# Quantised feed-forward: the normalised row made by GpSimd one pass sooner, its maximum first on VectorE, statistics between the two products

## What is computed

```python
x = x + _L0_xattn_ref(_layernorm(x, axis=-1), ctx_512, L0_xattn_Wq, L0_xattn_Wkv, L0_xattn_Wo)
x = x + _L0_attn_ref(_layernorm(x, axis=-1), L0_attn_w_attn, ...)
x = x + _L0_ffn_ref(_layernorm(x, axis=-1), L0_ffn_w_gate, L0_ffn_w_up, L0_ffn_w_down)
x = x + _L1_xattn_ref(_layernorm(x, axis=-1), ctx_512, ctx_512, ...)
x = x + _L1_attn_ref(_layernorm(x, axis=-1), L1_attn_W, L1_attn_b)
x = x + _L1_ffn_ref(_layernorm(x, axis=-1), ...)          # 34 experts
```

```python
def _act_quant(x):
    scale = 127.0 / jnp.clip(jnp.max(jnp.abs(x), axis=-1, keepdims=True), 1e-05)
    xq = jnp.clip(jnp.round(x * scale), -128.0, 127.0) / scale
    return x + jax.lax.stop_gradient(xq - x)
def _bitlinear(x, w):
    return jnp.einsum('bsi,oi->bso', _act_quant(x), _weight_quant(w))
gate = jax.nn.silu(_bitlinear(x, w_gate))
up = _bitlinear(x, w_up)
return _bitlinear(gate * up, w_down)
```

## Time and profile before

| | |
|---|---|
| median of three runs | 1316.04 us (1314.11 to 1318.54) |
| profiled execution | 1316.23 us, span 1314.1 us |
| granted TensorE clock, mean over the span | 0.977 |
| TensorE busy (matmuls) | 1207.7 us, 92% of the span |
| VectorE busy | 800.6 us, 61% |
| ScalarE busy | 645.4 us, 49% |
| GpSimd busy | 559.3 us, 43% |
| quantised feed-forward, first maximum of `h` to the last addition to `X` | about 404.8 to 512.8 us |

### The profile page before, as it was taken

How to read it: one execution, slowest core, us unless ns; L and a number is a source line. 1 busy time by engine, 2 the same in 40 slices (tenths; PEclk the granted TensorE clock), 3 DMA queues, 4 the chain that set the end, 5 groups by cost and what they waited for, 6 DMA issues and landing times. The chain is left out here.

```text
span 1314.1 us, 30226 instructions
## 1 busy us (share of the span) xinstructions
PE 1207.7 (92%) x9768; PEld 949.2 (72%) x9776; DVE 800.6 (61%) x1775; ACT 645.4 (49%) x1374; POOL 559.3 (43%) x824
## 2 busy tenths in 40 slices
PE   6899999989996778988886899999999999999998
PEld 5677777767774446866664688888888788888886
DVE  4688888857766883658885854444444444444443
ACT  5766666634445885544444333444443443333443
POOL 2244444467774443547775233333332233333331
PEclk9999999989999997999997899999999999999999
DMA  8200000000001000200000133333333433333331
GB/s 280 57 17 16 16 16 8 2 1 1 0 0 33 0 1 26 72 1 2 0 0 25 61 124 112 108 110 107 111 110 111 133 112 112 112 111 107 110 109 57
DMA packets 34042, 81.89 MB, mean 62 GB/s; under 512 B 4356, under 2 KB 11524, under 8 KB 33992
## 3 DMA queue, kind: packets, MB, share of 16 engines
q1 hardware_dynamic: 32808, 79.95, 18.7%
q10 hardware_dynamic: 1184, 1.31, 0.3%
HBM read 78.87 MB, written 2.38 MB: 62 GB/s over the span
## 5 line engine op out<-in xcount | busy, mean ns | idle before, releaser
L2275 POOL TENSOR_TENSOR sw<-sg,wb 128x512 f32<-128x512 f32 x136 | 176.4, 1297 | 399.1 <-ACT sg L2174 384.1
L2229 DVE TENSOR_TENSOR a<-sw,ps 128x512 f32<-128x512 f32 x136 | 93.6, 688 | 234.7 <-POOL sw L2275 234.6
L2179 ACT ACTIVATE ah<-a 128x512 fp32r<-128x512 f32 x136 | 86.0, 632 | 288.2 <-DVE a L2229 279.3
L2102 PE MATMUL ps<-Hh,wh 128*128 128x512 f32 x544 | 216.2, 397 | 2.3 <-DVE wl L2215 2.3
L2104 PE MATMUL ps<-Hh,wl 128*128 128x512 f32 x544 | 214.3, 394 | 0.0
L2103 PE MATMUL ps<-Hl,wh 128*128 128x512 f32 x544 | 213.3, 392 | 0.0
L658 ACT ACTIVATE Pr<-ps,mx 128x256 f32<-128x256 f32 x256 | 104.1, 480 | 61.0 <-DVE mx L559 61.0
L2233 DVE TENSOR_TENSOR al<-a,ah 128x512 fp32r<-128x512 f32 x136 | 94.2, 693 | 62.6 <-ACT ah L2179 59.2
L2102 PEld LDWEIGHTS ps<-Hh,wh 128*128 128x128 f32 x544 | 102.8, 189 | 25.3 <-issue 3.4
L2104 PEld LDWEIGHTS ps<-Hh,wl 128*128 128x128 f32 x544 | 102.8, 189 | 24.2
L2103 PEld LDWEIGHTS ps<-Hl,wh 128*128 128x128 f32 x544 | 102.9, 189 | 23.0
(11 more groups left out here) (232 smaller groups left out, 2431.1 us busy)
## 6 DMA issues: line engine op xcount, KB each, us to landing
wb<-token_weights SPq DMA_DIRECT2D x66, 512.0 KB, 3.6
raw<-in_ew SPq DMA_DIRECT2D x68, 384.0 KB, 3.0
cT<-in_ctxT SPq DMA_DIRECT2D x16, 256.0 KB, 2.7
cx<-in_ctxT SPq DMA_DIRECT2D x15, 256.0 KB, 2.8
X<-in_x SPq DMA_DIRECT2D x1, 1536.0 KB, 7.1
wqkv<-in_wqkv SPq DMA_DIRECT2D x2, 768.0 KB, 5.4
raw3g<-in_wg SPq DMA_DIRECT2D x1, 1024.0 KB, 5.4
raw3u<-in_wu SPq DMA_DIRECT2D x1, 1024.0 KB, 7.4
```

Of the source, the lines that this page charges most:

```text
L2102: eng.matmul(ps[:, bank, :], wh[:, u, w], HhT[:, c, cols], start=(c == 0), stop=False)
L2229: eng.tensor_tensor(a[:, tt, :], sw[:, tt, :], ps[:, UB[tt], :], ALU.mult).then_inc(m_a, 1)
L2275: eng.tensor_tensor(sw[:, tt, :], sg[:, tt, :], wb[:, u, tt * UT:(tt + 1) * UT], ALU.mult).then_inc(m_sw, 1)
```

## The change

In `quantised_ffn` alone:

- VectorE no longer makes `h` for this layer. Its pass i is now: `front1` of tile i+2, first half of `mul` of tile i, `ln_dve` of tile i+3, second half of `mul`, `amax2`.
- GpSimd makes `h` in a new step `centred`, with the same arithmetic, straight behind `ln_pool`, and both are done for tile i+3 in pass i, one pass sooner than before. Its pass i is now: `round1` and `scales` of i+2, `add_x` of i-2, `ln_pool` and `centred` of i+3, `scale2` of i. It makes `h` of the next layer's tile 0 too, in pass 13.
- `centred` waits for its own power, and for the maximum of tile i-2 counted from its own tile, which is the last reader of that buffer on VectorE.
- GpSimd's passes 0 to 15 are all written out (`each_pair`); the other engines keep the loop.

```diff
--- before.py
+++ after.py
@@ -1218,8 +1218,9 @@
 
     g = env
     sb, sem, ps, X = g["sb"], g["sem"], g["ps"], g["X"]
-    ln_dve, ln_dve2, ln_pool = g["ln_dve"], g["ln_dve2"], g["ln_pool"]
+    ln_dve, ln_pool = g["ln_dve"], g["ln_pool"]
     ln_h, s_xdone, h, ident = g["ln_h"], g["s_xdone"], g["h"], g["ident"]
+    lnmv, lnrs, ln_rs = g["lnmv"], g["lnrs"], g["ln_rs"]
     wg, wu, wd = g["wq3"]
     wsc = g["wsc"]
     L = 2
@@ -1251,6 +1252,17 @@
 
         return not isinstance(i, int) or low <= i <= high
 
+    def each_pair(body):
+
+        for i in range(-2, 0):
+            body(i, i % 2)
+        yield
+        for i in range(0, NPAIR):
+            body(i, i % 2)
+        yield
+        for i in range(NPAIR, NPAIR + 2):
+            body(i, i % 2)
+
     def pairs(eng, body):
 
         for i in range(-2, 0):
@@ -1375,22 +1387,17 @@
 
         def body(i, u):
             v = 1 - u
+            if within(i, -2, last - 2):
+                front1(i + 2, u)
             if within(i, 0, last):
                 mul(i, u, 0)
-                mul(i, u, 1)
-                amax2(i, u)
-            if within(i, -1, last - 2):
-                reach(eng, f_r, i + 1)
-                ln_dve2(eng, L, i + 2, u, f_r)
-            elif isinstance(i, int) and i == last - 1:
-                eng.wait_ge(f_r, i + 1)
-                ln_dve2(eng, L + 1, 0, u, f_r)
-            if within(i, -2, last - 2):
-                front1(i + 2, u)
             if within(i, -2, last - 3):
                 ln_dve(eng, L, i + 3, v)
             elif isinstance(i, int) and i == last - 2:
                 ln_dve(eng, L + 1, 0, v)
+            if within(i, 0, last):
+                mul(i, u, 1)
+                amax2(i, u)
 
         yield from pairs(eng, body)
 
@@ -1465,25 +1472,35 @@
             reach(eng, f_y, i - 1)
             eng.tensor_tensor(dq2[:, u, :], wsc[:, 2:3], ac2[:, u, :], ALU.mult).then_inc(f_dq2, 1)
 
+        def centred(n, i, u):
+
+            eng.wait_ge(ln_rs, NPAIR * n + i + 1)
+            reach(eng, f_am, i - 1 if n == L else NPAIR - 1)
+            eng.nop(nofuse=True)
+            eng.tensor_scalar(h[:, u, :], X[:, i, :], lnmv[:, u, 0:1], lnrs[:, u, :],
+                              ALU.subtract, ALU.mult).then_inc(ln_h, 1)
+
         def add_x(t, u):
             eng.wait_ge(f_y, t + 1)
             eng.tensor_tensor(X[:, t, :], X[:, t, :], y[:, u, :], ALU.add).then_inc(s_xdone, 1)
 
         def body(i, u):
             v = 1 - u
-            if within(i, -1, last - 2):
-                ln_pool(eng, L, i + 2, u)
-            elif isinstance(i, int) and i == last - 1:
-                ln_pool(eng, L + 1, 0, u)
-            if within(i, 2, last + 2):
-                add_x(i - 2, u)
-            if within(i, 0, last):
-                scale2(i, u)
             if within(i, -2, last - 2):
                 round1(i + 2, u)
                 scales(i + 2, u)
-
-        yield from pairs(eng, body)
+            if within(i, 2, last + 2):
+                add_x(i - 2, u)
+            if within(i, -2, last - 3):
+                ln_pool(eng, L, i + 3, v)
+                centred(L, i + 3, v)
+            elif isinstance(i, int) and i == last - 2:
+                ln_pool(eng, L + 1, 0, v)
+                centred(L + 1, 0, v)
+            if within(i, 0, last):
+                scale2(i, u)
+
+        yield from each_pair(body)
 
     return {"tensor": tensor, "vector": vector, "scalar": scalar, "gpsimd": gpsimd}
 
```

## The result

The changed kernel takes 1332.53 us (median of four runs, 1329.98 to 1341.68) against 1315.07 us for the kernel before (median of four): a ratio of 1.0143 with a 95% interval of 1.0086 to 1.0199. It is slower by some 17 us where 4.5 us faster was forecast, outside the forecast's range of 1309.3 to 1315.0 us.

The account below looks back on a forecast made before the run. VectorE was taken as the bound at 5.32 us a tile. Both ways put `xqT` of tile 15 at 484.7 us instead of 489.16: 4.5 us saved, median 1311.5, range 1309.3 to 1315.0 us.

Parts of the forecast that it names:

- way one: ScalarE with TensorE sets the pace: 12 tiles at 4.83 us put `xqT` of tile 15 at 484.7 us.
- Part (2): VectorE's new order costs 0.1 us; a loop pair takes about 10.1 us, or 5.05 a pass.
- Way two: VectorE sets the pace: first product of pass 2 at 425.2 us, `xqT` of tile 15 at 484.7.
- Part (3): `h` on GpSimd takes 0.5 us, ready 0.5 us or more before VectorE wants it; cost nothing.
- Part (4): Maximum one pass sooner: TensorE's 7.8 us of waits for `r` ahead of `xt` vanish; no cost.
- rival (E): VectorE's wait for GpSimd's `h` replaces the removed one; 1315 to 1317 us with an unfavourable phase; chance 0.10.
- (D): Rival: TensorE's clock stays low after the opening, 1.37 us a tile; 1314.3 to 1321 us; chance 0.06.
- Part (5): Opening: pass 0 begins with `front1` of tile 2, so `xqT` of tile 2 loses 0.4 us (0 to 1).
- Part (6): GpSimd's passes written out: no branch there, and GpSimd had slack, so no effect.
- Part (7): Closing: all behind `ar` of tile 14 moves as one block; 0, within 1 us for the clock.

Follow-up runs that it names:

- old-order kernel: Against the changed kernel: `h` stays on GpSimd, one pass sooner, but VectorE does both products first and GpSimd's order changes too; 1308.91 us, 0.9957 of before.
- with `dq` moved: Against the changed kernel: GpSimd's `scales` (the factors `dq`) moved from straight behind `round1` to behind `h`; 1313.37 us, 0.9997 of before.

## Why the prediction was wrong, point by point

**What bounded the kernel before: right.** VectorE led, with ScalarE and TensorE close behind at 4.83 us a tile. The old-order kernel shows both: VectorE is rid of `h`, 0.45 us a pass, and the stretch goes from 62.9 to 57.9 us, where way one of the sum gave 12 x 4.83 = 58.0.

**Part (2), VectorE's reordering: the size right, its use in the sum too kind.** Its own pass in the new order is 5.05 us in the loop, measured with `dq` moved. Way two of the sum still met way one's 58.0 us for the stretch, since it started VectorE ahead by more than a microsecond; with `dq` moved the stretch is 60.1, and the one wait of 1.5 us at 433.37 took about that much. 5.05 is 0.2 us a tile more than ScalarE's 4.83: the new order can't reach what the old one reaches with the same `h`.

**Part (3), the queue on GpSimd: the step that failed.** It wrote the chain to `h` from an `add_x` that ends 2.2 us after the first product, a distance read in the old order, and named what stands behind `centred`, but not what stands ahead of it. Ahead stands `scales`, with a wait whose target is the second product of tile i. In the rows of before that wait left no trace, because the products came first; only the code shows it. From the first product the forecast had `add_x` over at +2.2 us, `h` there at +3.6 and wanted at +4.1; in the turn shown above they are +3.4, +5.6 and +3.8. The slack of 0.5 to 1 us was a shortage of 1.8: the wait put `add_x` back by 1.2 us, and from there to the end of `h` its size and gap added 0.9. The diff moves the second product behind the maximum, so every wait on the products' semaphore had to be looked up again.

**Part (3), the size of `h`: mis-sized as well.** 0.5 was taken, with 0.73 as the upper end, a row of another operation that bounds nothing here; it is 1.23 us and 0.21 of gap. The nearest row, `r`, multiplies and adds; `h` subtracts first. By itself this cost nothing: with the queue free or with the old order, 1.23 us is hidden. Inside the turn it puts in 0.9 us more than was taken (an estimate from the links; the runs took out at most 0.33). Without these a tile would take 6.73 - 0.9 = 5.8 us, still more than 5.37 before, so the forecast fails by the wait alone. The run with `h` on VectorE, 0.45 us, agrees: the order still loses 0.24 us a tile (5.61 against 5.37).

**Part (4), `xt` no longer waits for `r`: right, and of no use.** The rival (E), the wait for GpSimd's `h` in place of the one removed, is what happened, with its sign in the trace exactly as named (idle time of VectorE ahead of its maximum, ended by `h`, in every pass of the loop). It was given 0.10 and priced by the size of `h` alone, 1315 to 1317 us, without the wait that carries it. Its bound for the size was sound: `h` would have to take 1.5 us to be felt, and with the queue free 1.44, gap included, are not. The rule that it takes from the Trainium skill ("SBUF — State Buffer", Who interferes with whom), a VectorE instruction with two SBUF inputs contending with a GpSimd one that reads SBUF, stayed out of play: `r` still takes 482 ns, and `h` 1227 ns with VectorE idle (changed) and 1226 beside VectorE's work (`dq` behind `h`). Of (D), the lower clock after the opening, there is no sign: `at` of tile 1 and later takes 1.04 to 1.09 us.

**Part (5), the opening: too dear.** 0.4 us was taken off; in the changed kernel, where the clock of the opening was full as before (1.00 from 404 to 415 us), `xqT` of tile 3 came at 426.10 against 426.28, so nothing was lost.

**Part (6): right. Part (7):** the closing moved as one block, to 1.0 us (22.9 us before, 21.9 after), but the profiled execution paid 10 us for the clock behind it, ten times the 1 us allowed.

With the queue free, the stretch gains 2.8 us of the 4.9 that the sum gave it (62.9 to 58.0), while the median stands at 0.9997 (0.9985 to 1.0009), between a gain of 2.0 us and a loss of 1.2. The clock hides the rest: in executions with a mean clock of 0.977 to 0.979 this kernel took 1312.21 to 1313.79 us (seven, median 1313.4) and the kernel before 1315.40 to 1318.76 (nine, median 1316.2), which is again 2.8 us. Why its clock was the lower one more often is open.

## What to carry to other kernels

When an instruction is moved, list every wait that counts it, in the lines that the diff leaves alone too: a wait that never shows in the trace may be hidden only by the order that is given up. Then follow the queue behind the instruction that waits; here a 0.3 us step of three columns held back the normalisation of a whole tile. Last, the size of a moved step matters only if it lies in the turn: 1.23 us cost nothing in one order and counted in full in another.

## What the runs showed of the hardware

GpSimd's `tensor_scalar` on 128x256 float32 depends on the pair of operations: multiply and add 482 ns (one pointer scalar) to 553 ns (two), subtract and multiply 1154 ns (one) to 1227 ns (two). The second pointer costs 70 ns in either, the pair of operations 670. (The forms that subtract also read the mean as a pointer from `lnmv`, the others don't; the runs don't part the two.) On VectorE subtract and multiply takes 0.41 us. "GPSIMD Engine Reference" of the Trainium skill, Engine selection, has one-input elementwise work roughly at line rate on GpSimd; these runs agree for multiply and add only.

TensorE's granted clock goes with 3 to 10 us of a single execution of this kernel: 0.56 to 0.58 or 1.00 in the same 11 us of the opening, and 0.50 or 1.00 in the next layer behind an equally slow stage. Gains of 2 or 3 us were visible in the pace between two fixed instructions, or among executions with the same mean clock, and not reliably in the medians of all.
